# Gathering per-item adapters by indirect DMA, and another order of weight chunks, in an adapter and mixture-of-experts kernel

## The chip, the cores and the metric
One core of one Trainium2 chip runs the whole program. The metric is the device time of one execution in microseconds (us). It is lower when the kernel is better.

## The reference
The input is `x` of 64 items by 64 tokens by 256 features, float32, with two ids per item. What is computed, in order:

```
# L0: adapter
h   = gelu(x @ down_W.T + down_b)                 # 256 -> 64, erf gelu
h   = h @ expert_W[id].T + expert_b[id]           # one 64x64 adapter per item (16 adapters,
h   = h + domain_emb[id]                          #   or the identity for an invalid id)
x1  = layernorm(h @ up_W.T + up_b + x) * gamma + beta
# L1: style-conditioned mixture of experts
n   = layernorm(x1) * ln_g + ln_b
n   = (n - mean over the item's tokens) * rsqrt(var over the item's tokens)
sty = mlp(subj_emb[subject_id])                   # 64->128->128->64->512
n   = n * softplus(sty[:256]) + sty[256:]
top 2 of 8 experts by softmax(n @ router_w), gates normalised over the two
out = x1 + sum of the two of gate * (relu(n @ w1[e] + b1[e]) @ w2[e] + b2[e])   # 256->1024->256
```

## The kernel before, in words
The 4096 tokens go through a **front** in 8 groups of 512 tokens (8 items each), and then the expert layers run over **tiles** of up to 256 routed tokens (32 whole tiles and 7 half ones). The front ends where the first twelve tiles are known and their tokens lie in the DRAM tensor `queues`. A short stretch of groups 6 and 7 runs beside the first tiles.

The front is a software pipeline written out by hand, with one instruction list for each engine. `iterations(body)` runs `body` for i = 0 to 7, and `back(i, n)` is the group n iterations earlier. Iteration i does the adapter of group i, the layer norms of group i-1 (`s2`), the item norm, router and top-2 of group i-2 (`s3`), and place numbers and scatter of group i-3 (`s4`). An engine's list is strictly in order: an instruction that waits holds up all behind it on its engine.

The **expert weights** are 32 chunks of 128 x 1024 float32 (512 KB). A chunk is loaded by SP into one of four slots of `stage` (`load_weights`, L447 to L450), ScalarE writes its high half in f16 (`cut_high`, L916), and VectorE the rest (`cut_low`, L1246). SP loads chunk q when `w_low_ready` has reached q-3: chunk q-4 has to be cut by VectorE first. `CUTS` (L57) says how many chunks belong to each iteration; the last entry is the stretch behind iteration 7. In iterations 1 to 7 VectorE cuts its chunks behind `norm_shift` of group i-1. ScalarE cuts the first one ahead of `activate`, the second ahead of `adapted`, and all others ahead of `item_norm` of group i-2, which the router (PE `route`), the logits copy (ACT `logits`) and VectorE's `best_two` follow.

The **adapters** of all 64 items are made at the start: the table of 17 x 4096 is loaded, and PE's `select` (L650) multiplies it by a one-hot matrix in 32 steps. The copies (`copy_selected`) lie between the chunk cuts on ScalarE and VectorE and bring it into `wsel`. `scratch`, `table` and `wsel` lie in the room of weights that come late. The **style net** (`style_layer`, `style_out`, `softplus`, `item_gammas`) runs once, in iteration 1 and right behind it.

GpSimd does the powers of the norms (`rstd`, `item_rstd`) and the scatters: eight indirect DMAs for each group from iteration 3 on, two ahead of the second `rstd` and six behind it.

PE's order in `body` is `into_features`, `adapter` (down, adapters, up), `route`, `back_rows`, `normed_into_features`, `rank`. SP's order is the chunks of iteration i, `load_x` for group i+1 once `up_done` of group i-1 is there, and `store_x1` of group i-1.

Of the kernel before, what the change touches and what calls it, by code (L numbers as in the profile page):

```python
# [26 lines left out]
F32 = mybir.dt.float32  # L27
# [7 lines left out]
P = 128  # L35
# [21 lines left out]
CUTS = [8, 3, 3, 3, 3, 3, 3, 3, 3]  # L57
# [5 lines left out]
W2_AT = EXPERTS * DC * FF  # L63
STAGES = 4
# [80 lines left out]
def program(nc, sem, env):  # L145
# [11 lines left out]
    with ExitStack() as ctx:  # L157
# [6 lines left out]
        part_no = sb("part_no", [P, 1])  # L164
        expert_no = sb("expert_no", [P, EXPERTS])
# [63 lines left out]
        table = w_low[0:NONE_ROW + 1, 16 * CHUNK:24 * CHUNK].bitcast(F32)  # L229
        wsel = w_low[0:A, 24 * CHUNK:32 * CHUNK].bitcast(F32)  # L230
        wsel_pairs = wsel.rearrange("a (i q w) -> a w q i", q=A // 2, w=2)
# [7 lines left out]
        idf = scr(NONE_ROW + 1, ITEMS)  # L239
        sidf = scr(SUBJECTS, ITEMS)  # L240
        idc = scr(NONE_ROW + 1, ITEMS)
# [18 lines left out]
        ids_i = scr(SUBJECTS, ITEMS).bitcast(I32)  # L260
# [57 lines left out]
        ids_loaded, table_loaded = sem("ids_loaded"), sem("table_loaded")  # L318
# [3 lines left out]
        hot_ready, select_done = sem("hot_ready"), sem("select_done")  # L322
        select_copied = [sem("select_copied0"), sem("select_copied1")]
# [26 lines left out]
        N_EARLY, N_LATE = 8, 8  # L350
        N_POOL = 13
        SELECTS = A // 16

        def iterations(body, after={}):

            for i in range(GROUPS):
                body(At(i // 2, i % 2))
                if i in after:
                    after[i]()
# [73 lines left out]
        with nc.Block() as block:  # L433

            @block.sync
            def _(sp):
# [17 lines left out]
                sp.dma_start(ids_i, spread(ids, SUBJECTS)).then_inc(ids_loaded, 16)  # L454
                sp.dma_start(sids_i, spread(subject_ids, SUBJECTS)).then_inc(ids_loaded, 16)
                for dst, src in ((dw[:], down_w), (t_ab, adapter_b), (t_de, domain_emb), (t_se, subj_emb),
                                 (ab[:, 0:1], down_b), (ab[:, 1:2], sty_b1), (uw[0:A], up_w), (uw[A:A + 1], up_b)):
                    sp.dma_start(dst, src).then_inc(early_loaded, 16)
                load_weights(At(0, 0), slice(0, 2))
# [3 lines left out]
                def body(i):  # L463
# [1196 lines left out]
```

## Time and profile before

| what | value |
|---|---|
| time, median of 3 runs | 590.06 us (589.53 to 590.67) |
| the profiled execution | 590.25 us, span 588.4 us |
| PE busy | 535.2 us, 91% |
| VectorE busy | 380.0 us, 65% |
| ScalarE busy | 277.2 us, 47% |
| GpSimd busy | 244.2 us, 42% |
| DMA, mean over the span | 57.58 MB, 98 GB/s |
| first expert matmul of PE (L835) | starts at 181.35 us |

The span runs from the first to the last instruction; the time holds some 1.9 us more around it. A busy share is taken over the whole span, and the front (up to 181 us) and the expert tiles have different limits, so the share of PE says little about the front.

### The profile page before, as it was taken

Reading aid. Unit: us, or ns where it says so; the run is one execution under the profiler, and the core shown is the slowest. Engines: PE = TensorE matmul, PEld = TensorE weight load, DVE = VectorE, ACT = ScalarE, POOL = GpSimd, SP = SyncE. Lnnn points to the kernel's source line nnn. Section 1 sums busy time; section 2 is a strip of 40 time slices with the busy share of each in tenths; the row PEclk is TensorE's granted clock in tenths of the full one; section 3 lists DMA queues with packets and bytes.
Section 4 is the critical chain, followed back from the end, with each engine's and each line's share of the span. In section 5 each row is a group of like instructions: output and inputs, shape, how many; then the busy total and the mean of one; then the engine's idle time right before and its main releaser. Section 6 shows DMA issues by size and latency. Waiting matters only on the chain.

```text
span 588.4 us, 15554 instructions
## 1 busy us (share of the span) xinstructions
PE 535.2 (91%) x4386; PEld 450.1 (76%) x4387; DVE 380.0 (65%) x1233; ACT 277.2 (47%) x628; POOL 244.2 (42%) x208
## 2 busy tenths in 40 slices
PE   5987887879886999999999999999999999999991
PEld 4755654665655988888888888888888888887781
DVE  2475989888889868558865464554645546464541
ACT  3547766766663663444243342534425334254430
POOL 2000458888776625647233242322423223233222
PEclk9778789786967999899999999999999999999997
DMA  9466355775354343435655234342333424324411
GB/s 243 149 204 180 104 157 171 252 236 183 145 191 112 80 64 46 103 65 112 135 92 72 38 46 62 39 69 36 49 59 40 68 36 50 49 35 52 45 27 19
DMA packets 78094, 57.58 MB, mean 98 GB/s; under 512 B 51346, under 2 KB 71699, under 8 KB 77907
## 3 DMA queue, kind: packets, MB, share of 16 engines
q1 hardware_dynamic: 63698, 38.37, 25.6%
q0 software_dynamic: 13296, 17.83, 18.0%
q10 hardware_dynamic: 1058, 0.85, 0.7%
q8 instruction: 22, 0.36, 0.3%
q14 instruction: 20, 0.16, 0.1%
HBM read 23.18 MB, written 24.55 MB: 81 GB/s over the span
## 4 chain that ended last, share of the span: by engine, by line
PE 65%; POOL 12%; DVE 8%; issue 7%; DMA 4%; ACT 2%; SPq 1%; POOLq 0%; DVEq 0%; ACTq 0%
PE banks L835 28%; PE banks L851 27%; POOL queues L573 5%; POOL rsT L581 3%; DMA out<-nb,token 3%; PE banks L658 2%; POOL rs L564 2%; PE banks L718 2%; DVE stats L1172 2%; PE banks L719 1%; DVE w_low L1255 1%; POOL out L604 1%; PE banks L698 1%; DMA uw<-up_b 1%; PE banks L693 1%
## 5 line engine op out<-in xcount | busy, mean ns | idle before, releaser
L604 POOL DMA_INDIRECT out<-nb,token x71 | 115.6, 1628 | 224.1 <-ACT nb L1046 199.9
L835 PE MATMUL banks<-rT,w_high 128*128 128x256 f16 (+1 forms) x1248 | 198.5, 266 | 6.2 <-DMA rT<-queues 5.7
L851 PE MATMUL banks<-w_high,stage 128*128 x1136 | 188.2, 273 | 1.0 <-issue 0.5
L835 PE MATMUL banks<-rT,w_low 128*128 128x256 f16 (+1 forms) x624 | 164.2, 265 | 0.0
L851 PE MATMUL banks<-w_low,stage 128*128 x568 | 154.8, 273 | 0.0
L1030 ACT ACTIVATE xb<-banks,feat 128x256 f32<-128x256 f32 (+1 forms) x312 | 120.1, 453 | 52.3 <-PE banks L835 45.3
L835 PEld LDWEIGHTS banks<-rT,w_high 128*128 x1248 | 115.0, 99 | 25.5 <-issue 7.6
L851 PEld LDWEIGHTS banks<-w_high,stage 128*128 128x128 f16 x1136 | 110.5, 98 | 14.9 <-issue 2.3
L1046 ACT ACTIVATE nb<-act,gate 128x256 f32<-128x256 f32 x71 | 32.6, 501 | 178.7 <-DVE act L1513 174.6
L1488 DVE TENSOR_TENSOR stage<-xb,stage 128x512 f16<-128x512 f32 (+1 forms) x156 | 100.7, 646 | 5.4
L1486 DVE CAST stage<-xb 128x512 f16<-128x512 f32 (+1 forms) x156 | 67.0, 430 | 56.1 <-ACT xb L1030 54.8
L573 POOL DMA_INDIRECT queues<-h_rows,slot x64 | 75.6, 1182 | 22.5 <-issue 17.5
L1513 DVE SCALAR_TENSOR_TENSOR act<-banks,b 128x256 f32<-128x256 f32 x71 | 27.2, 420 | 86.7 <-PE banks L851 83.0
L835 PEld LDWEIGHTS banks<-rT,w_low 128*128 x624 | 61.5, 99 | 6.5
L851 PEld LDWEIGHTS banks<-w_low,stage 128*128 128x128 f16 x568 | 55.6, 98 | 6.4
L1255 DVE SCALAR_TENSOR_TENSOR w_low<-stage,w_high 128x1024 f16<-128x1024 f32 x32 | 37.6, 1222 | 2.8 <-ACT w_high L919 2.8
L562 POOL TENSOR_SCALAR rs<-mv 128x4 f32<-128x4 f32 x16 | 5.1, 319 | 71.5 <-DVE mv L1177 71.2
L919 ACT ACTIVATE w_high<-stage 128x1024 f16<-128x1024 f32 x32 | 33.4, 1052 | 2.5 <-DMA stage<-expert_w 2.5
L581 POOL TENSOR_TENSOR rsT<-varT,minus_half 128x8 f32<-128x8 f32 x16 | 27.0, 1699 | 15.6 <-DVE varT L1215 15.6
L718 PE MATMUL banks<-uw,dom 65*128 65x256 f32 x64 | 27.0, 513 | 4.8 <-ACT dom L938 4.8
L719 PE MATMUL banks<-xb,ident 128*128 128x256 f32 x64 | 25.7, 492 | 0.0
L944 ACT ACTIVATE hT<-hT,aff_c,aff_a 128x64 f32<-128x64 f32 x56 | 19.3, 427 | 7.1 <-DVE aff_c L1232 7.1
(186 smaller groups left out, 521.9 us busy)
## 6 DMA issues: line engine op xcount, KB each, us to landing
stage<-expert_w SPq DMA_DIRECT2D x32, 512.0 KB, 4.4
xb<-x SPq DMA_DIRECT2D x8, 512.0 KB, 6.1
out<-rb SPq DMA_DIRECT2D x8, 512.0 KB, 3.2
queues<-pad_row SPq DMA_DIRECT2D x9, 260.0 KB
out<-nb,token POOLq DMA_INDIRECT x71, 4.0
queues<-h_rows,slot POOLq DMA_INDIRECT x64
b<-exp_b SPq DMA_DIRECT2D x1, 1024.0 KB, 6.7
rT<-queues SPq DMA_TRANSPOSE x39
```

The costliest lines, as they stand in the source:

```text
L573: nc.gpsimd.indirect_dma_start(out=queues, out_offset=bass.IndirectOffsetOnAxis(ap=slot[:, i.par, t, k:k + 1], axis=0), in_=h_rows[:, i.pa ...
L581: nc.gpsimd.tensor_tensor(rsT[:, of_c], varT[:, of_c], minus_half[:, of_c], ALU.pow).then_inc(rsT_ready, 1)
L604: nc.gpsimd.indirect_dma_start(out=out, out_offset=bass.IndirectOffsetOnAxis(ap=token[:, i.par, s:s + 1], axis=0), in_=yg[:, i.par, s, :], ...
L718: nc.tensor.matmul(ps_u[:, t, :], dom[:, t * P:(t + 1) * P], uw[:], start=True, stop=False)
L835: last = nc.tensor.matmul(ps_in(i, c), w[:, at], features(i)[:, v, k, :], start=(n == 0), stop=(n == 3 * DC - 1))
L851: last = nc.tensor.matmul(ps_out(i.par)[:, s, :], v[:, i.par, c, s * P:(s + 1) * P], w[:, at], start=(n == 0), stop=(n == 3 * FC - 1))
L919: nc.scalar.activation(w_high[:, bass.ds(q * CHUNK, CHUNK)], stage[:, slot], ACT.Copy, scale=WSCALE).then_inc(w_high_ready, 1)
L1030: last = nc.scalar.activation(hid[:, c, 0:i.rows], ps_in(i, c), ACT.Relu, scale=1.0 / WSCALE, bias=feat[:, bass.ds(e * FC + (B1 + c), 1)])
L1046: nc.scalar.activation(yg[:, i.par, s, :], yb[:, s, :], ACT.Copy, scale=gate[:, i.par, s:s + 1]).then_inc(gated, 1)
L1255: V.scalar_tensor_tensor(w_low[:, w], stage[:, slot], WSCALE, w_high[:, w], ALU.mult, ALU.subtract).then_inc(w_low_ready, 1)
L1486: V.tensor_copy(hid_high[:, i.par, s, r], hid[:, s, r]).then_inc(split_high, 1)
L1488: V.tensor_tensor(hid_low[:, i.par, s, r], hid[:, s, r], hid_high[:, i.par, s, r], ALU.subtract).then_inc(split_low, 1)
```

## The change
1. **Adapters.** `select`, its one-hot table load and its eight copies go. VectorE works out for each of 128 partitions which row of the adapter table (1088 rows of 64) it wants (`row_no`). GpSimd gathers with 32 indirect DMAs of 128 rows of 256 B: four for each group (`GATHERS`), 16 ahead of iteration 0, 8 at the end of iterations 1 and 2 each. PE turns a group's four blocks (`turn_rows`), ScalarE copies the bank into `wsel` (`copy_adapters`).
2. **Loads.** The ids come first on ScalarE's queue. SP loads group 0's tokens, the small weights and then waits for the gathers of group 0 ahead of the first chunk. In iterations 1 and later SP loads the tokens ahead of the chunks, the first three chunks of an iteration ahead of `store_x1`, and the others behind it.
3. **Chunks** by iteration: 7, 6, 5, 3, 2, 2, 2, 2, and 3 behind, for 8 and then 3 each.
4. **Style.** VectorE's `style_out` goes ahead of `cut_low`, ScalarE's `softplus` ahead of `scale_features` and the last cuts of iteration 1, and `item_gammas` into iteration 2. The Gelu table is loaded explicitly at the start and behind `softplus`.

```diff
-CUTS = [8, 3, 3, 3, 3, 3, 3, 3, 3]
+CUTS = [7, 6, 5, 3, 2, 2, 2, 2, 3]
...
 # SP
                 load_x(At(0, 0))
...
+                sp.wait_ge(rows_loaded[0], GATHERS * 16)
                 load_weights(At(0, 0), slice(0, 2))
                 load_x(At(0, 1))
                 load_weights(At(0, 0), slice(2, STAGES))
...
-                    load_weights(i, slice(STAGES if i.g == 0 else 0, None))
-                    if (s2 := back(i, 1)) is not None:
-                        if i.g + 1 < GROUPS:
-                            sp.wait_ge(up_done, s2.g + 1)
-                            load_x(At(s2.half + 1, s2.par))
+                    s2 = back(i, 1)
+                    if s2 is not None and i.g + 1 < GROUPS:
+                        sp.wait_ge(up_done, s2.g + 1)
+                        load_x(At(s2.half + 1, s2.par))
+                    load_weights(i, slice(STAGES if i.g == 0 else 0, 3 if i.g else None))
+                    if s2 is not None:
                         store_x1(s2)
+                        load_weights(i, slice(3, None))
 # GpSimd
+                def gather(g):
+                    for n in range(g * GATHERS, (g + 1) * GATHERS):
+                        nc.gpsimd.indirect_dma_start(
+                            out=wrows[:, n * A:(n + 1) * A], out_offset=None, in_=table_rows,
+                            in_offset=bass.IndirectOffsetOnAxis(ap=row_no[:, n:n + 1], axis=0)).then_inc(rows_loaded[g], 16)
+                pool.wait_ge(rows_known, 2)
+                for g in range(4):
+                    gather(g)
...
+                    if i.g == 1 or i.g == 2:
+                        gather(2 * i.g + 2)
+                        gather(2 * i.g + 3)
 # PE
+                def turn_rows(g):
+                    pe.wait_ge(rows_loaded[g], GATHERS * 16)
+                    wait(pe, adapters_copied, g)
+                    if g == 2:
+                        pe.wait_ge(net_ready, 5)
+                    wait(pe, low_ready, g - 3)
+                    for k in range(GATHERS):
+                        n = g * GATHERS + k
+                        last = nc.tensor.transpose(banks[0:A, 4, k * PAIR:(k + 1) * PAIR], wrows[:, n * A:(n + 1) * A],
+                                                   ident[:])
+                    last.then_inc(rows_turned, 1)
...
 # PE, adapter(i): group 0 does the down matmuls first, then
                     if i.g == 0:
-                        select()
...
+                        item_rows()
+                        turn_rows(0)
...
+                        add_item_rows()
...
                     adapter(s1)
+                    if i.g + 1 < GROUPS:
+                        turn_rows(i.g + 1)
 # ScalarE
+                def copy_adapters(g):
+                    sc.wait_ge(rows_turned, g + 1)
+                    nc.scalar.activation(wsel[:, g * GI * A:(g + 1) * GI * A], banks[0:A, 4, :],
+                                         ACT.Copy).then_inc(adapters_copied, 1)
...
                     if i.g == 0:
+                        activate(s1)
+                        copy_adapters(0)
+                        adapted(s1)
+                        cut_high(i, slice(0, 4))
+                        copy_adapters(1)
+                        cut_high(i, slice(4, None))
+                        return
+                    if i.g == 1:
                         cut_high(i, slice(0, 1))
                         activate(s1)
...
+                        cut_high(i, slice(1, 2))
                         adapted(s1)
...
+                        cut_high(i, slice(2, 3))
+                        layer_norm(s2)
+                        softplus()
+                        nc.scalar.preload_act_table(ACT.Gelu)
+                        scale_features(s2)
+                        cut_high(i, slice(3, None))
+                        copy_adapters(2)
                         return
...
                     cut_high(i, slice(2, None))
                     if s3 is not None and s3.g < FIRST:
                         item_norm(s3)
+                    if 1 < i.g < GROUPS - 1:
+                        copy_adapters(i.g + 1)
                     if s2 is not None:
                         layer_norm(s2)
 # VectorE
+                link(V.tensor_copy(idf, ids_i))
+                link(V.tensor_scalar(idc, idf, -1.0, float(NONE_ROW), ALU.max, ALU.min))
+                link(V.tensor_scalar(none, idc, 0.0, float(NONE_ROW + 1), ALU.is_lt, ALU.mult))
+                link(V.tensor_tensor(idc, idc, none, ALU.add))
...
+                    V.tensor_scalar(row_no[some], of_half, part_share[some, 0:1], float(A), ALU.add,
+                                    ALU.mult).then_inc(rows_known, 1)
...
                     if i.g == 0:
-                        cut_low(i, slice(0, 1))
-                        for b in range(SELECTS):
-                            copy_selected(b)
-                            cut_low(i, slice(b + 1, b + 2))
                         row_constants()
-                        cut_low(i, slice(SELECTS + 1, None))
+                        cut_low(i, slice(None))
                         return
...
+                    if i.g == 2:
+                        item_gammas()
...
                     step(s2, norm_shift)
+                    style_step(style_out)
                     cut_low(i, slice(None))
-                    style_step(style_out)
...
-                iterations(body, after={1: item_gammas})
+                iterations(body)
```

## Rows read from the trace of the kernel before

**Rows 1.** Busy time of PE, PEld, VectorE, ScalarE, GpSimd in a stretch (start:end length), granted clock, DMA

```profile
95.10:113.70 18.60, 15.49 (x85) 12.24 (x86) 16.85 (x70) 12.17 (x24) 16.17 (x15) 0.82 0.63 212
...
132.40:152.90 20.50, 18.41 (x89) 12.55 (x88) 17.19 (x72) 12.77 (x24) 17.45 (x17) 0.72 0.59 205
...
181.30:588.00 406.70, 391.76 (x3652) 345.19 (x3652) 240.69 (x720) 168.15 (x449) 148.72 (x101) 0.98 0.39 61
```

**Rows 2.** Timeline of VectorE: start us, duration, line, operation

```profile
8.65 0.18 DVE L1114 CAST w_high<-w_high 17x64 f32<-17x64 int32 x1 [7.29 <-DMA w_high<-subject_ids]
...
39.40 1.43 DVE L1172 BATCH_NORM_STATS2 stats<-banks 128x6 f32<-128x256 f32 x4 [1.71 <-PE banks L719]
...
48.33 0.16 DVE L1199 SCALAR_TENSOR_TENSOR shift<-mv,rs 128x4 f32<-128x4 f32 x1 [1.47 <-POOL rs L564]
...
51.81 0.47 DVE L1155 TENSOR_SCALAR w_high<-banks,feat 128x64 f32<-128x64 f32 x2
...
59.03 1.43 DVE L1172 BATCH_NORM_STATS2 stats<-banks 128x6 f32<-128x256 f32 x4
...
69.73 0.16 DVE L1199 SCALAR_TENSOR_TENSOR shift<-mv,rs 128x4 f32<-128x4 f32 x1 [0.33 <-POOL rs L564]
...
73.22 0.37 DVE L1262 MAX8 top<-lg 128x8 f32<-128x8 f32 x4
...
76.40 1.42 DVE L1172 BATCH_NORM_STATS2 stats<-banks 128x6 f32<-128x256 f32 x4
...
107.12 3.50 DVE L1255 SCALAR_TENSOR_TENSOR w_low<-stage,w_high 128x1024 f16<-128x1024 f32 x3
```

**Rows 3.** Timeline of TensorE, same columns

```profile
13.08 1.94 PE L693 MATMUL banks<-ident,item_add 128*64 128x512 f32 x2 [0.53 <-DVE w_high L1128]
...
18.02 11.20 PE L658 MATMUL banks<-w_high,w_low 17*128 17x64 f32 x64
...
33.27 1.22 PE L718 MATMUL banks<-uw,dom 65*128 65x256 f32 x2 [0.68 <-ACT dom L938]
...
38.77 0.59 PE L719 MATMUL banks<-xb,ident 128*128 128x256 f32 x2
...
146.59 0.96 PE L719 MATMUL banks<-xb,ident 128*128 128x256 f32 x2
```

**Rows 4.** Timeline of ScalarE, same columns

```profile
18.71 1.04 ACT L919 ACTIVATE w_high<-stage 128x1024 f16<-128x1024 f32 x1
...
32.63 0.59 ACT L938 ACTIVATE dom<-banks 64x512 f32<-64x512 f32 x1 [2.07 <-PE banks L710]
...
53.52 1.45 ACT L978 ACTIVATE hT<-banks,feat 128x512 f32<-128x512 f32 x2 [2.92 <-PE banks L753]
...
54.86 0.31 ACT L910 ACTIVATE w_high<-w_high 128x128 f32<-128x128 f32 x1
...
58.10 0.31 ACT L914 ACTIVATE w_high<-w_high 128x128 f32<-128x128 f32 x1
...
66.79 2.76 ACT L944 ACTIVATE hT<-hT,aff_c,aff_a 128x64 f32<-128x64 f32 x8 [0.94 <-DVE aff_c L1232]
...
69.93 2.08 ACT L964 ACTIVATE nb<-rb,shift,rs 128x256 f32<-128x256 f32 x4 [0.38 <-DVE shift L1199]
```

**Rows 5.** Timeline of GpSimd, iteration 4, behind the second rstd

```profile
107.17 2.13 POOL L573 DMA_INDIRECT queues<-h_rows,slot  x1 [0.20 <-issue]
...
109.61 1.86 POOL L573 DMA_INDIRECT queues<-h_rows,slot  x1 [0.30 <-issue]
...
111.77 0.96 POOL L573 DMA_INDIRECT queues<-h_rows,slot  x1 [0.31 <-issue]
```

**Rows 6.** DMA issues: size, median us from issue to landing

```profile
out<-nb,token POOLq DMA_INDIRECT x71, 4.0
...
w_high<-subject_ids SPq DMA_DIRECT2D x1, 8.0 KB, 6.9
```

**Rows 7.** Source line L450, the 32 chunk loads

```profile
DMA to landing us min/median/max: 3.2/4.4/9.0
```

More of the change, by code:

```diff
@@ L63 @@
 W2_AT = EXPERTS * DC * FF
+ROWS_AT = CHUNKS - GROUPS // 2
+ADAPTERS_AT = ROWS_AT - GROUPS
+PAIR = 2 * A
+GATHERS = GROUP // T // 2
 STAGES = 4
@@ L259, in program @@
         lnz = scr(P, DC * ITEMS)
[L260 removed]
+        ids_i = scr(P, ITEMS).bitcast(I32)
         sids_i = scr(SUBJECTS, ITEMS).bitcast(I32)
@@ L648, in item_rows @@
                     nc.tensor.matmul(banks[0:SE, 7, A:A + ITEMS], t_se, hot_s, start=True, stop=True).then_inc(net_done, 1)
-                def select():
-                    pe.wait_ge(table_loaded, 32)
-                    for b in range(SELECTS):
-                        for w in range(2):
-                            wait(pe, select_copied[w], b - 1)
-                        for k in range(8):
-                            q = b * 8 + k
-                            last = nc.tensor.matmul(banks[:, 4 + b % 2, k * ITEMS:(k + 1) * ITEMS],
-                                                    table[:, q * 2 * A:(q + 1) * 2 * A], hot_w, start=True, stop=True)
-                        last.then_inc(select_done, 1)
+                def turn_rows(g):
[9 more added lines that the diff above has]
+                    last.then_inc(rows_turned, 1)
                 def style_layer(k):
@@ L1013, in body @@
                         scale_features(s2)
-                sc.dma_start(table[0:ADAPTERS], adapter_w[0:ADAPTERS]).then_inc(table_loaded, 16)
-                sc.dma_start(table[ADAPTERS:NONE_ROW + 1].rearrange("o (k n) -> o k n", k=16),
-                             adapter_w[ADAPTERS:NONE_ROW + 1].rearrange("o (k n) -> o k n", k=16)).then_inc(table_loaded, 16)
-                for dst, src in ((hw1, hyp_w1), (feat[:], feature), (hw2, hyp_w2), (sw1, sty_w1), (sw2, sty_w2),
-                                 (g0[:], spread(gamma0, P)), (b0[:], spread(beta0, P)), (rw[:], router_w)):
-                    sc.dma_start(dst, src).then_inc(late_loaded, 16)
-                iterations(body, after={1: softplus})
+                sc.dma_start(ids_i, spread(ids, P)).then_inc(ids_loaded, 16)
+                sc.dma_start(sids_i, spread(subject_ids, SUBJECTS)).then_inc(ids_loaded, 16)
+                nc.scalar.preload_act_table(ACT.Gelu)
+                for dst, src in ((t_ab, adapter_b), (t_de, domain_emb), (t_se, subj_emb), (ab[:, 1:2], sty_b1)):
+                    sc.dma_start(dst, src).then_inc(early_loaded, 16)
+                iterations(body)
                 cut_high(last_chunks, slice(None))
@@ L1447, in body @@
                     step(s3, row_fields)
-                iterations(body, after={1: item_gammas})
+                iterations(body)
                 def late_tiles():
```

100 lines of the change are left out of this document (47 added, 53 removed).

## The prediction

> **What bounds the kernel now.** I read the stretches first. In the expert tiles TensorE is busy 391.8 of 406.7 us at a granted clock of 0.98 [rows 1]; the change touches no tile, so this part is fixed and the question is only when it starts. The front gives that start: PE's first tile matmul waits for tokens that SP fetches once VectorE has the table of tiles, and VectorE makes this table at the end of iteration 7. So I follow VectorE's list through the front. I mark an iteration by the first `stats` of group i-1 (L1172): iteration 1 begins at 39.40, 2 at 59.03, 3 at 76.40 [rows 2], and 4 at the left edge of the stretch 95.1:113.7 [rows 1].
>
> Three different limits show. Up to 39.40 it is one chain: VectorE has the ids at 8.65 [rows 2], PE's `select` takes 11.20 us from 18.02, the last copy into `wsel` ends at 29.25 + 1.30 = 30.55 [rows 3, 4], then come the adapter matmuls, ScalarE's copy `dom` at 32.63, and the sixteen up matmuls from 33.27 [rows 3, 4]. In iterations 1 and 2 it is VectorE's own list with one wait for the softplus. From iteration 4 on GpSimd has no rest: 16.17 us busy in 18.60 [rows 1], and the eight gaps of 0.30 us between its scatters [rows 5] are issue time, not waiting. VectorE is nearly as full (16.85) and waits for GpSimd's second power once in each iteration.
>
> The sum is made against the profiled execution, 590.25 us; the median of the runs, 590.06, lies 0.2 us lower.
>
> **The start (to iteration 1).** `select` and its copies go. The gathers take their place, and all of the following is in series.
> - Ids: 6.9 us from issue to landing [rows 6], issued some 0.5 us earlier (two issues ahead of it on SP fall away). By that 8.1; as the table load no longer shares the queues, it can be sooner. I take 7.5 (5.2 to 8.1).
> - Six small VectorE operations of 0.18 and a little [rows 2]: 1.3, so 8.8.
> - Four gathers. No gather is in the trace. The nearest row is a scatter of 128 rows: 0.96 us by itself, 2.13 beside a chunk cut, 0.30 between two [rows 5]. No cut runs yet, so I take 0.96: 4 x 0.96 + 3 x 0.30 = 4.7, so 13.6. Bounds 0.96 and 2.13 each.
> - Landing: the indirect DMA of the tiles takes 4.0 us from its issue [rows 6]; from the last gather's issue at 12.6 that is 16.6; its own issue is shorter, so I take 16.0.
> - PE turns the four blocks (1.0 at half clock) and adds the item rows, 1.94 [rows 3]: 18.9. ScalarE's copy of 0.6, of the shape of `dom` [rows 4], lies beside it.
> - From here as before: 30.55 to 39.40, 8.85 us: `up_done` at 27.8.
> - New behind it: `turn_rows(1)` 0.5, `copy_adapters(1)` 0.6, and ScalarE's last three cuts of iteration 0, which now stand behind that copy, 3 x 1.04 [rows 4], and VectorE's last cut 1.2 (3.50 for three [rows 2]). Iteration 1 begins at 33.2.
>
> That is 6.2 us sooner than 39.40. The chunks themselves start late, since SP waits for group 0's gathers (16.0 where it was 6.6), but a load takes 3.2 to 4.4 us [rows 7] and ScalarE is not free for the first cut before 21.6; this wait is covered. SP has the first four chunks and the tokens of group 1 behind it, and PE needs those only after 27.8.
>
> **Iteration 1 (6 chunks for 3).** It was 59.03 - 39.40 = 19.6, with VectorE idle for the softplus. Now VectorE has `style_out` ahead of the cuts (two pairs of 0.47 [rows 2]) and no wait there, but ScalarE makes chunks 10 to 12 only behind the whole style chain. Path: `norm_shift` 48.33 - 39.40 = 8.95 [rows 2]; `layer_norm` 2.3 with its start; softplus from 54.86 to 58.41, 3.55; the Gelu table 1.28; `scale_features` 1.45; three cuts 3.1 [rows 4]; VectorE's last one 1.2. Sum 21.8: **+2.2**.
>
> **Iteration 2 (5 chunks for 3).** Here I expect the main loss. Chunks 13 to 17; a chunk's load waits until the chunk four before it is cut by VectorE. So 13 to 16 come early, but 17 waits for VectorE's cut of 13, which stands behind `norm_shift`. And ScalarE's `item_norm`, `layer_norm`, `logits` and `high` stand behind its cut of 17. Before, `item_norm` ran at 66.79, 3 us ahead of `norm_shift` at 69.73 [rows 2, 4]. Now: `norm_shift` at 10.7 plus 0.6 for `item_gammas`, 11.3. Then VectorE's cut 1.2, load 4.0 (3.2 to 4.4 [rows 7]), ScalarE's cut 1.04, `item_norm` 2.76, `copy_adapters` 0.6, `layer_norm` 2.1, the logits copy 0.2, and VectorE from `best_two` to the next `stats` 76.40 - 73.22 = 3.2 [rows 2, 4]. That is 15.2, where it was 76.40 - 69.73 = 6.7. The iteration is 26.5 for 17.4: **+9.1** (bounds 8.3 to 13, the longest loads and a half-clock PE for the router).
>
> **Iteration 3** has 3 chunks as before; `copy_adapters` takes 0.6 us in front of `layer_norm` where ScalarE had idled 1.4 us for VectorE's shift: **+0.1**. PE's `turn_rows`, 0.5 us, lies in PE's wait for `item_norm`.
>
> **Iterations 4 to 6 (2 chunks for 3).** VectorE saves 1.17 each. GpSimd sets the pace: beside 3.50 us of cuts two scatters took 2.13 + 1.86 instead of 2 x 0.96 [rows 2, 5], 2.07 lost, 0.6 us for each us of cuts. A third less is 0.7. **-0.7 each, -2.1** (bounds 0 to -1.17 each). **Iteration 7**: VectorE saves 1.17, but GpSimd's last scatters, which SP waits for also, save only 0.7: **-0.9**.
>
> The gathers of iterations 1 and 2, eight each behind the second `rstd`: 8 x 1.26 = 10.1, and 0.6 x 3.5 for the cuts beside them, twice at most: 14.3. They start 9.0 into iteration 1 and end by 23.3; the next `rstd` is due 1.9 into iteration 2, 23.7. Cost 0, by a hair.
>
> The shared port gets a rule in the Trainium skill (page "SBUF — State Buffer", section "SBUF: two separate sides"): a VectorE instruction that holds the port pair blocks GpSimd fully, not in part. The rows give 0.6, not 1. By the rule the gathers of iteration 1 would lose 7.0 instead of 4.2.
>
> **Sum.** -6.2 + 2.2 + 9.1 + 0.1 - 2.1 - 0.9 = **+2.2**: 592.4 for the profiled execution, about 592.3 for the median. Slower.
>
> **Rivals.**
> 1. *The start gains more than the stalls cost* (faster). Its place is the chain to 33.2. If the ids land at 5.2 (-2.3), and PE is at the full clock for the up matmuls (two take 0.59 at 38.77 against 1.22 at 33.27 [rows 3], so 3.5 for 6.1, -2.6) and for the turn (-0.5), iteration 1 begins at 27.8 and the time is 592.4 - 5.4 = 587.0. It decides if iteration 1 begins before 31 us. For it: the queue is lighter. Against it: PE rests from 12 to 16 us and was at half clock after such rests.
> 2. *The slow stretch goes.* Iteration 6 took 20.5 us at a granted clock of 0.72 [rows 1]: its up matmuls ended at 147.55 and ScalarE waited for the router. If the clock falls elsewhere, the iteration is 18.0 and gains 2.5 instead of 0.7: 590.6, no change that can be told.
> 3. *The new copy makes the slow stretch worse.* `layer_norm` now stands behind `copy_adapters`, which waits for PE behind its up matmuls. With those ending at 147.55 [rows 3]: turn 1.0, copy 0.6, `layer_norm` 2.1, so the logits copy at 151.3 instead of 149.3, +2.1, and the 0.7 is lost also: 592.4 + 2.8 = 595.2.
> 4. *GpSimd is late with its gathers.* At a full block in iteration 1 (both sets of three cuts, 7.0 us) the gathers end at 26.1 into it, 2.4 after the next `rstd` is due: 594.8. For it: one gather's price is unknown. (It is the port rule above that gives this.)
>
> **How the numbers follow.** Forecast 0.42, rival 1 0.25, rival 2 0.15, rival 3 0.12, rival 4 0.06. A change below 0.2%, 1.2 us, can't be told from none here. The forecast, rivals 3 and 4 are slower, 0.60, less the forecast's low edge of 0.02; rival 2 with that edge is 0.17; rival 1 is 0.25. The forecast's own range is 590.8 to 595. The whole range takes in rival 1's 587.0 and rival 3's 595.2 with the unknown prices of the load and the gather (3 us up if each gather of the first group takes 2.13 and a chunk load longer): 586 to 598.
>
> **What would show it.** In the changed trace: iteration 1's `stats` near 33 us (before 31: rival 1). In iteration 2 ScalarE idle for a chunk load, `item_norm` some 6 us behind `norm_shift` instead of ahead; `stats` of iteration 3 near 81.5, later than 76.40. Iterations 4 and 5 near 18.0 us long. If `item_norm` of group 0 isn't behind the shift, the main term is wrong. If GpSimd's `rstd` starts later than VectorE's moments in iteration 2, rival 4 holds.

## The result, and the profile after

The changed kernel takes 595.50 us (median of 5 runs, 591.68 to 599.32), the kernel before 589.74 us beside it (5 runs, 588.94 to 590.67). The ratio is 1.010, with a 95% interval of 1.0066 to 1.0133: slower, by 5.8 us in the medians. The forecast was 592.3, in a range of 586 to 598. All ratios here and below compare fast executions only; four of the 70 of the kernel before in the experiments were slow ones and stand in its medians, but not in the ratios.

The profiled execution of the changed kernel is the longest of its five, 599.32 us, and its span is 9.1 us longer than the span before. I compare the two fronts first. The marks are the same as in the prediction: an iteration begins at the first `stats` of VectorE, and the front ends at the first tile matmul.

| begins at (us) | it. 1 | it. 2 | it. 3 | it. 4 | it. 5 | it. 6 | it. 7 | first tile | end of span |
|---|---|---|---|---|---|---|---|---|---|
| before | 39.4 | 59.0 | 76.4 | 95.1 | 113.7 | 132.4 | 152.8 | 181.35 | 588.4 |
| after | 33.0 | 57.7 | 85.8 | 104.4 | 123.3 | 140.9 | 158.45 | 186.30 | 597.5 |
| after - before | -6.4 | -1.3 | +9.4 | +9.4 | +9.6 | +8.5 | +5.7 | +4.95 | +9.1 |

The front is 4.95 us longer, and that is near the 5.8 us between the medians. The other 4.2 us lie in the tiles (411.2 us for 407.0), which the change doesn't touch. In the ten profiled runs of the experiments, all with the same instructions in the tiles, this part took 406.6 to 410.8 us, 409.1 in the mean. About half of the 4.2 us is thus the spread of single executions. The other half, by which that mean lies above 407.0, may be spread of the one profile of before: the kernel before with nothing but the new chunk numbers also took 409.25. Whether any of it belongs to the change is open.

The page of the changed kernel, with its busy times, three of its groups (busy us, mean ns of one, idle before and what ended it) and the chunk loads (KB each, us to landing):

```profile
span 597.5 us, 15538 instructions
PE 527.9 (88%) x4354; PEld 443.4 (74%) x4355; DVE 376.0 (63%) x1233; ACT 275.4 (46%) x631; POOL 274.8 (46%) x240
L1302 DVE SCALAR_TENSOR_TENSOR w_low<-stage,w_high 128x1024 f16<-128x1024 f32 x32 | 37.7, 1220 | 20.0 <-ACT w_high L953 20.0
L597 POOL DMA_INDIRECT w_low<-adapter_w,row_no x32 | 34.8, 1088 | 13.1 <-issue 9.2
L953 ACT ACTIVATE w_high<-stage 128x1024 f16<-128x1024 f32 x32 | 33.1, 1050 | 15.1 <-DMA stage<-expert_w 15.1
stage<-expert_w SPq DMA_DIRECT2D x32, 512.0 KB, 5.4
```

The L953 row is the first hint. ScalarE was idle for 15.1 us because a chunk had not landed, 10.3 of them in iteration 2. VectorE was idle for 20.0 us because ScalarE had not cut; 10.2 of these lie ahead of its very first cut. GpSimd has 30.6 us more work than before, and no wait of that kind stands at it.

The timeline of VectorE after, which answers to [rows 2] (start, duration, line, operation, idle before):

```profile
6.62 0.20 DVE L1163 CAST w_high<-w_high 128x64 f32<-128x64 int32 x1 [4.90 <-DMA w_high<-subject_ids]
...
32.98 1.42 DVE L1220 BATCH_NORM_STATS2 stats<-banks 128x6 f32<-128x256 f32 x4
...
41.35 0.28 DVE L1197 TENSOR_SCALAR w_high<-banks,ab 64x64 f32<-64x64 f32 x1 [2.68 <-PE banks L694]
...
44.83 0.16 DVE L1247 SCALAR_TENSOR_TENSOR shift<-mv,rs 128x4 f32<-128x4 f32 x1 [1.48 <-POOL rs L574]
...
54.28 3.50 DVE L1302 SCALAR_TENSOR_TENSOR w_low<-stage,w_high 128x1024 f16<-128x1024 f32 x3 [5.12 <-ACT w_high L953]
57.70 1.41 DVE L1220 BATCH_NORM_STATS2 stats<-banks 128x6 f32<-128x256 f32 x4
...
68.93 0.16 DVE L1247 SCALAR_TENSOR_TENSOR shift<-mv,rs 128x4 f32<-128x4 f32 x1 [0.33 <-POOL rs L574]
69.01 4.62 DVE L1302 SCALAR_TENSOR_TENSOR w_low<-stage,w_high 128x1024 f16<-128x1024 f32 x4
75.11 1.23 DVE L1302 SCALAR_TENSOR_TENSOR w_low<-stage,w_high 128x1024 f16<-128x1024 f32 x1 [1.48 <-ACT w_high L953]
81.64 0.37 DVE L1309 MAX8 top<-lg 128x8 f32<-128x8 f32 x4 [5.29 <-ACT lg L985]
...
84.26 1.23 DVE L1334 TENSOR_TENSOR h_rows<-banks,h_rows 128x1024 f16<-128x1024 f32 x1 [0.88 <-ACT h_rows L992]
```

Two waits stand out. In iteration 1 VectorE is idle for 5.12 us, until ScalarE comes to the last three chunks. In iteration 2 it is idle for 5.29 us, until the logits are there. ScalarE shows why (answers to [rows 4]):

```profile
30.75 1.06 ACT L953 ACTIVATE w_high<-stage 128x1024 f16<-128x1024 f32 x1 [0.61 <-DMA stage<-expert_w]
...
51.86 1.45 ACT L1012 ACTIVATE hT<-banks,feat 128x512 f32<-128x512 f32 x2
53.20 2.94 ACT L953 ACTIVATE w_high<-stage 128x1024 f16<-128x1024 f32 x3
...
69.21 1.06 ACT L953 ACTIVATE w_high<-stage 128x1024 f16<-128x1024 f32 x1 [6.58 <-DMA stage<-expert_w]
74.03 1.06 ACT L953 ACTIVATE w_high<-stage 128x1024 f16<-128x1024 f32 x1 [3.76 <-DMA stage<-expert_w]
74.99 2.75 ACT L978 ACTIVATE hT<-hT,aff_c,aff_a 128x64 f32<-128x64 f32 x8
...
81.41 0.20 ACT L985 ACTIVATE lg<-banks 128x32 f32<-128x32 f32 x1 [1.23 <-PE banks L763]
```

The three cuts of iteration 1 (53.20) stand behind the whole style chain and `scale_features` (51.86). In iteration 2 the cut at 74.03 is chunk 17's. Its load could be issued only when VectorE had cut chunk 13, the first of the four at 69.01. `item_norm` (L978) stands behind it at 74.99, where before it ran at 66.79, ahead of VectorE's shift [rows 4].

Chunk 16, the cut at 69.21, was late as well, for another reason. The change puts the fourth and fifth chunk of an iteration behind `store_x1` in SP's list, and the store of group 1 waits until VectorE has finished the group's first layer norm. SP after:

```profile
64.52 0.40 SPq L450 DMA_DIRECT2D out<-rb  x1
64.95 5.63 SPq L455 DMA_DIRECT2D stage<-expert_w  x2
```

The second row holds the loads of chunk 16, at 64.95, and of chunk 17, at the end of its 5.63 us. Chunk 12, whose slot chunk 16 takes, was cut at 57.8, so the load of 16 waited some 7 us for the store. Without chunk 17 `item_norm` would still have stood behind this cut, at 70.3, though ScalarE was free from 62.6 on and VectorE had the last of its coefficients at 67.8. By these rows the place of the store would then cost 2.5 us or more; that is my estimate.

PE after (answers to [rows 3]):

```profile
14.90 1.06 PE L684 MATMUL banks<-ident,w_low 128*64 128x128 f32 x4 [4.25 <-DMA w_low<-adapter_w,row_no]
...
26.00 0.60 PE L684 MATMUL banks<-ident,w_low 128*64 128x128 f32 x4
...
35.12 0.66 PE L694 MATMUL banks<-w_high 128*128 128x64 f32 x2 [6.37 <-DVE w_high L1191]
...
37.47 3.62 PE L726 MATMUL banks<-xT,dw 128*64 128x512 f32 x4
...
77.79 3.58 PE L763 MATMUL banks<-rw,hT 128*128 128x8 f32 x16 [7.82 <-ACT hT L978]
```

Both long rows, 37.47 and 77.79, come behind a rest of PE (6.37 and 7.82 us). The same work of the same group in the kernel before took half as long, so these rows are at the lower of TensorE's two levels, 1.2 GHz, and those of before at 2.4:

```profile
42.80 1.88 PE L698 MATMUL banks<-xT,dw 128*64 128x512 f32 x4
...
70.21 1.85 PE L732 MATMUL banks<-rw,hT 128*128 128x8 f32 x16
```

GpSimd after (answers to [rows 5]):

```profile
8.37 1.20 POOL L597 DMA_INDIRECT w_low<-adapter_w,row_no  x1 [3.90 <-DVE row_no L1170]
...
12.39 0.95 POOL L597 DMA_INDIRECT w_low<-adapter_w,row_no  x1 [0.30 <-issue]
...
59.62 0.23 POOL L572 TENSOR_SCALAR rs<-mv 128x4 f32<-128x4 f32 x1 [3.29 <-DVE mv L1225]
...
69.08 2.12 POOL L597 DMA_INDIRECT w_low<-adapter_w,row_no  x1 [0.18 <-issue]
71.50 1.82 POOL L597 DMA_INDIRECT w_low<-adapter_w,row_no  x1 [0.30 <-issue]
...
116.57 2.11 POOL L583 DMA_INDIRECT queues<-h_rows,slot  x1 [0.20 <-issue]
118.99 0.97 POOL L583 DMA_INDIRECT queues<-h_rows,slot  x1 [0.30 <-issue]
```

And the stretches of iterations 2, 4, 5, 6 and of the tiles after, with the columns of [rows 1]:

```profile
57.70:85.80 28.10, 17.62 (x84) 14.64 (x83) 19.66 (x72) 13.87 (x24) 15.90 (x14) 0.64 0.49 167
...
104.40:123.30 18.90, 16.30 (x90) 12.01 (x90) 15.85 (x70) 11.99 (x24) 16.17 (x16) 0.82 0.44 145
123.30:140.90 17.60, 14.71 (x90) 10.83 (x90) 15.84 (x71) 12.04 (x25) 14.44 (x14) 0.90 0.69 239
140.90:158.40 17.50, 14.72 (x90) 10.83 (x90) 15.73 (x69) 11.95 (x24) 15.07 (x15) 0.90 0.54 175
...
186.30:597.50 411.20, 394.48 (x3652) 347.07 (x3652) 239.34 (x719) 168.69 (x449) 148.08 (x100) 0.97 0.38 60
```

No engine is full in iteration 2: VectorE, the busiest, has 19.66 of 28.10 us. It is a stretch of waits, and the granted clock is 0.64 in it.

### The profile page after: what moved, and what is told of

It reads as the page before. It is cut to its first block, busy times and chain, and to the rows that moved or that the text cites. A ratio compares the mean times of both kernels' runs of the same rounds, so it can differ in the third digit from the quotient of the medians.

```text
span 597.5 us, 15538 instructions
## 1 busy us (share of the span) xinstructions
PE 527.9 (88%) x4354; PEld 443.4 (74%) x4355; DVE 376.0 (63%) x1233; ACT 275.4 (46%) x631; POOL 274.8 (46%) x240
## 4 chain that ended last, share of the span: by engine, by line
PE 59%; POOL 12%; DVE 9%; issue 7%; DMA 7%; ACT 4%; SPq 0%; ACTq 0%; POOLq 0%; DVEq 0%
PE banks L869 28%; PE banks L885 27%; POOL queues L583 5%; DMA out<-nb,token 3%; POOL rsT L591 3%; DMA stage<-expert_w 3%; POOL rs L574 2%; DVE w_low L1302 2%; DVE stats L1220 2%; POOL out L628 1%; PE banks L763 1%; DMA w_high<-subject_ids 1%; PE banks L726 1%; POOL rs L572 1%; PE banks L749 1%
## 5 line engine op out<-in xcount | busy, mean ns | idle before, releaser
L869 PEld LDWEIGHTS banks<-rT,w_high 128*128 x1248 | 115.4, 99 | 28.1 <-issue 9.4
L885 PEld LDWEIGHTS banks<-w_high,stage 128*128 128x128 f16 x1136 | 110.5, 98 | 14.7 <-issue 1.9
L583 POOL DMA_INDIRECT queues<-h_rows,slot x64 | 72.5, 1133 | 22.5 <-issue 17.2
L1558 DVE SCALAR_TENSOR_TENSOR act<-banks,b 128x256 f32<-128x256 f32 x71 | 27.1, 420 | 87.6 <-PE banks L885 85.9
L597 POOL DMA_INDIRECT w_low<-adapter_w,row_no x32 | 34.8, 1088 | 13.1 <-issue 9.2
L953 ACT ACTIVATE w_high<-stage 128x1024 f16<-128x1024 f32 x32 | 33.1, 1050 | 15.1 <-DMA stage<-expert_w 15.1
L749 PE MATMUL banks<-uw,dom 65*128 65x256 f32 x64 | 29.5, 557 | 5.9 <-ACT dom L972 4.1
L750 PE MATMUL banks<-xb,ident 128*128 128x256 f32 x64 | 27.7, 527 | 0.0
L749 PEld LDWEIGHTS banks<-uw,dom 65*128 65x128 f32 x64 | 17.4, 283 | 10.5 <-ACT dom L972 5.0
```

The lines of the kernel that those rows point to most:

```text
L583: nc.gpsimd.indirect_dma_start(out=queues, out_offset=bass.IndirectOffsetOnAxis(ap=slot[:, i.par, t, k:k + 1], axis=0), in_=h_rows[:, i.pa ...
L597: nc.gpsimd.indirect_dma_start(out=wrows[:, n * A:(n + 1) * A], out_offset=None, in_=table_rows, in_offset=bass.IndirectOffsetOnAxis(ap=ro ...
L749: nc.tensor.matmul(ps_u[:, t, :], dom[:, t * P:(t + 1) * P], uw[:], start=True, stop=False)
L869: last = nc.tensor.matmul(ps_in(i, c), w[:, at], features(i)[:, v, k, :], start=(n == 0), stop=(n == 3 * DC - 1))
L885: last = nc.tensor.matmul(ps_out(i.par)[:, s, :], v[:, i.par, c, s * P:(s + 1) * P], w[:, at], start=(n == 0), stop=(n == 3 * FC - 1))
L953: nc.scalar.activation(w_high[:, bass.ds(q * CHUNK, CHUNK)], stage[:, slot], ACT.Copy, scale=WSCALE).then_inc(w_high_ready, 1)
```

## Experiments

Ten kernels. Each median stands beside that of the kernel before on the same chip. A single profiled execution differs from the next by 1 or 2 us in a mark even where the instructions up to it are the same (iteration 1 of the changed kernel began at 33.0, 34.0 and 34.3 in three such runs), so I read marks to about that.

### One chunk fewer in iteration 2

```diff
-CUTS = [7, 6, 5, 3, 2, 2, 2, 2, 3]
+CUTS = [7, 6, 4, 3, 3, 2, 2, 2, 3]
```

> The changed kernel with one chunk moved from iteration 2 to iteration 4: CUTS 7, 6, 4, 3, 3, 2, 2, 2, 3. Theory (the fifth chunk of iteration 2 can load only after VectorE has cut the first, and ScalarE's item_norm stands behind it): ScalarE no longer waits for the load of chunk 17, item_norm of group 0 starts near 70.3 us instead of 75.0, iteration 3 begins near 80 instead of 85.8, and iteration 4 is 0.9 longer. Time 590.5, some 5 us below the changed kernel's 595.5. Rival (the loss in iteration 2 is the amount of cutting on VectorE, or PE at half clock, whatever the order): one chunk, 1.2 us less in iteration 2, given back in iteration 4: 595.

Measured: 590.58 us (10 runs) for 590.46, ratio 1.0001 (0.9973 to 1.0028). Iteration 2 took 23.4 us (58.7 to 82.2) instead of 28.1. With four chunks the last load of the iteration waits for no cut behind the shift. Moving the fifth chunk brings the time back to that of the kernel before. It doesn't bring iteration 2 back to its 17.4 us: ScalarE still waits 5.38 us for chunk 16, whose load stands behind `store_x1`, and `item_norm` starts only at 71.4. No run here has that load ahead of the store with four chunks, so its price is open.

### The chunks as before, all the rest of the change kept

```diff
-CUTS = [7, 6, 5, 3, 2, 2, 2, 2, 3]
+CUTS = [8, 3, 3, 3, 3, 3, 3, 3, 3]
```

> The changed kernel with the old chunk numbers 8, 3, 3, 3, 3, 3, 3, 3, 3 and all else of the change. Theory: the gathers and the new load order gain some 6 us at the start and only the chunk numbers lose it again in iterations 1 and 2: iteration 2 begins near 51, iteration 3 near 70 (76.4 in the kernel before), later iterations are 0.9 longer than in the changed kernel: time 583.5, faster than before by some 6 us. Rival (what the change adds besides the chunks, the gathers on GpSimd, the turns on PE and the copies in ScalarE's list, eats the gain): 590 or more.

Measured: 588.96 us (10 runs) for 590.46, ratio 0.9979 (0.9948 to 1.001). The interval holds 1, so a gain isn't shown, and in the medians it is far smaller than I expected, 1.5 us. The profiled execution looks better: its first tile matmul comes at 175.88, 5.5 us sooner than before. But at 586.98 us it is one of the fastest of its ten runs. Iterations 2 and 3 took 22.0 and 20.7 us. VectorE and then GpSimd in this run:

```profile
53.34 1.67 DVE L1253 BATCH_NORM_STATS2 statsT<-hT 128x6 f32<-128x128 f32 x8 [1.76 <-ACT hT L1012]
58.32 1.67 DVE L1241 SCALAR_TENSOR_TENSOR rb<-rb,rs,b 128x256 f32<-128x256 f32 x4 [1.68 <-POOL rs L574]
...
78.35 1.67 DVE L1241 SCALAR_TENSOR_TENSOR rb<-rb,rs,b 128x256 f32<-128x256 f32 x4 [1.37 <-POOL rs L574]
```

```profile
55.94 0.94 POOL L597 DMA_INDIRECT w_low<-adapter_w,row_no  x1 [0.30 <-issue]
56.91 0.24 POOL L572 TENSOR_SCALAR rs<-mv 128x4 f32<-128x4 f32 x1
```

Iteration 1 is only 14.7 us long here (35.0 to 49.75), and the last gather ends at 56.88. The `rstd` that VectorE needs starts right behind it, at 56.91, with no idle time before it. (The first row above is another delay, ScalarE's `scale_features` behind the softplus.) This is rival 4's place, but not its cause: the gathers end about 22 us into iteration 1, near the 23.3 of the prediction's sum, but the iteration that had to cover them had become 10 us shorter.

### Chunk 17's high cut behind layer_norm in iteration 2

```diff
-                    cut_high(i, slice(2, None))
+                    cut_high(i, slice(2, 4 if i.g == 2 else None))
...
+                    if i.g == 2:
+                        cut_high(i, slice(4, None))
```

> The changed kernel with the same chunk numbers, but in iteration 2 ScalarE cuts the fifth chunk (17) behind layer_norm instead of ahead of item_norm. Theory (the order on ScalarE, not the number of chunks, makes the stall): item_norm starts near 70.3, the cut of 17 near 76, iteration 3 begins near 81.5 instead of 85.8: time 591. Rival (number of chunks): no difference, 595.

Measured: 591.32 us (10 runs) for 590.46, ratio 1.0035 (1.0003 to 1.0067); iteration 3 begins at 81.6, and iteration 2 took 23.3 us for 28.1. The number of chunks is the changed kernel's; only ScalarE's order differs. So these 4.8 us aren't the fifth chunk's work (1.04 us on ScalarE, 1.17 on VectorE), but `item_norm` behind a load that waits for VectorE. The iteration is still 5.9 us longer than before; ScalarE waits 4.89 us for chunk 16 here too, and `item_norm` starts at 70.8.

### Only the new chunks, on the kernel before

```diff
-CUTS = [8, 3, 3, 3, 3, 3, 3, 3, 3]
+CUTS = [7, 6, 5, 3, 2, 2, 2, 2, 3]
```

> The kernel before with the new chunk numbers 7, 6, 5, 3, 2, 2, 2, 2, 3 alone. Theory: in iteration 1 and in iteration 2 ScalarE's layer_norm or item_norm waits for chunks (12 and 17) that load only after VectorE's first cut of that iteration; two stalls of 7 to 9 us each, less 1 us at iteration 0 and 3 us in iterations 4 to 7: 600 to 605. Rival (front-loading is free by itself, and the loss comes with the gathers or the load order): 587 to 590.

Measured: 602.88 us (4 runs) for 590.46, ratio 1.0204 (1.0145 to 1.0262). Iteration 1 took 27.1 us and iteration 2 27.9. ScalarE in iteration 2:

```profile
82.38 1.06 ACT L919 ACTIVATE w_high<-stage 128x1024 f16<-128x1024 f32 x1 [9.08 <-DMA stage<-expert_w]
```

The same wait for the same chunk, without any gather in the program. Here all five loads stand ahead of the store, and only chunk 17 is late. In iteration 1 ScalarE waited 3.92 and 2.46 us for chunks 11 and 12. The table of chunks costs 12.4 us by itself; beside it the rest of the change gives 6 to 7 us back. The two don't simply add up: without the new table the rest gave only 1.5 us in the medians.

### Old chunks, gathers spread

Five groups are gathered ahead (for four), group 5 between the two `rstd` of iteration 1, groups 6 and 7 at the end of iterations 1 and 2.

```diff
-CUTS = [7, 6, 5, 3, 2, 2, 2, 2, 3]
+CUTS = [8, 3, 3, 3, 3, 3, 3, 3, 3]
...
-                for g in range(4):
+                for g in range(5):
...
+                    if i.g == 1:
+                        gather(5)
...
-                        gather(2 * i.g + 2)
-                        gather(2 * i.g + 3)
+                        gather(i.g + 5)
```

> The changed kernel with the old chunk numbers and the gathers placed otherwise: five groups ahead of iteration 0, one between the two rstd of iteration 1, one at the end of iterations 1 and 2 each (eight at the end of each before). Theory (in short iterations the eight gathers end after the next rstd is due, the mechanism of the prediction's rival 4: with old cuts VectorE waited for GpSimd 1.7 us in iteration 2 and 1.4 + 2.3 us in iteration 3): these waits go, iteration 3 begins near 70.3 instead of 71.8 and lasts 18.7 instead of 20.8, time 585.5, 3.5 below the 589.0 of the old cuts alone. Rival (the wait only hides another, ScalarE's late logits of group 0): 588 to 589.

Measured: 587.41 us (11 runs) for 589.63, ratio 0.9954 (0.9925 to 0.9983): faster than both kernels. GpSimd now idles ahead of the `rstd` of iteration 2:

```profile
55.75 0.23 POOL L572 TENSOR_SCALAR rs<-mv 128x4 f32<-128x4 f32 x1 [1.96 <-DVE mv L1226]
```

Iteration 3 takes 18.4 us (72.4 to 90.8) for 20.7 with all eight gathers at the end. Iteration 1 takes 17.9 for 14.7, as PE's up matmuls ran at the lower clock (two in 1.06 us, from 46.69 to 53.79) where they had run at the full one. In the profiled executions the first tile matmul comes only 0.4 us sooner than with the old chunks alone, and the intervals of the two ratios overlap. That the waits for GpSimd go is shown; that the spreading pays in time isn't. Its median lies 1.9 us above what I expected, and its first tile matmul comes 5.9 us sooner than before (175.49) for 2.2 us between the medians. The profiled execution, 583.98 us, is near the low end of its 11 runs (583.52 to 589.49), so its marks show more than the median gives. What makes single executions of one kernel differ by 6 us is open; the mean granted clocks of these 11 (0.932 to 0.948) don't order them by time.

### New chunks, gathers spread

The same edit of the gathers, on the changed kernel.

> The changed kernel with its own chunk numbers and the gathers placed as in the run before this one. Theory: with the new chunk numbers iterations 1 and 2 are so long that the gathers end before the next rstd is due (56.3 against 59.6, and 80.9 against 87.7 in the changed kernel), so nothing changes: 595. Rival (the gathers cost the changed kernel something, by the port or by DMA beside the chunk loads): 592 or less.

Measured: 595.52 us (6 runs) for 589.63, ratio 1.0115 (1.0065 to 1.0165), the changed kernel's own time (1.010). So in the changed kernel the gathers cost nothing on GpSimd, and rival 4 is out for it. Beside the run before this one, the chunks alone are worth 595.52 - 587.41 = 8.1 us.

### Old chunks, chunk loads ahead of the tokens again

```diff
-CUTS = [7, 6, 5, 3, 2, 2, 2, 2, 3]
+CUTS = [8, 3, 3, 3, 3, 3, 3, 3, 3]
...
+                    load_weights(i, slice(STAGES if i.g == 0 else 0, 3 if i.g else None))
                     if s2 is not None and i.g + 1 < GROUPS:
                         sp.wait_ge(up_done, s2.g + 1)
                         load_x(At(s2.half + 1, s2.par))
-                    load_weights(i, slice(STAGES if i.g == 0 else 0, 3 if i.g else None))
```

> The changed kernel with the old chunk numbers and, in iterations 1 and later, the first chunks loaded ahead of the tokens again. Theory (tokens are needed a whole iteration after they are asked for, so their order is covered): as with the old cuts alone, 589, iteration starts the same within 0.5 us. Rival (chunks that stand behind up_done come late to ScalarE): 1 to 3 us faster.

Measured: 590.15 us (11 runs) for 589.63, ratio 1.0019 (0.9984 to 1.0055). Against 0.9979 for the same kernel with tokens first the two intervals overlap. Inconclusive: what the order on SP is worth isn't told apart from nothing. The marks missed my 0.5 us: iteration 1 began at 35.15 for 35.02, but iteration 2 at 52.8 for 49.75. The up matmuls of iteration 1 ran at the lower clock here too. GpSimd shows something that the changed kernel doesn't, a gather that lasted through all that was left of three cuts (VectorE's, 47.25 to 50.73):

```profile
47.94 3.62 POOL L597 DMA_INDIRECT w_low<-adapter_w,row_no  x1 [0.30 <-issue]
```

### No wait for the rows ahead of the first chunk

```diff
-                sp.wait_ge(rows_loaded[0], GATHERS * 16)
```

> The changed kernel without SP's wait for the gathers of group 0 ahead of the first chunk; chunks and tokens of group 1 load from 7.7 us on. Theory (the wait costs nothing, as ScalarE has no time for the first cut before 20.3 us, and it keeps the gathers from sharing the DMA engines with 2.5 MB): the gathers of group 0 land 0 to 2 us later than 14.9 us, iteration 1 begins at 33 to 35, time 595 to 597. Rival (the late chunks hold up ScalarE's cuts 4 to 6 and so the start of iteration 1, where it idled 0.6 to 0.9 us before each): iteration 1 begins near 31, time 593.

Measured: 599.6 us (5 runs) for 589.63, ratio 1.0173 (1.0131 to 1.0215), and iteration 1 begins at 36.4. GpSimd's last gather of group 0 and then PE's first turn:

```profile
12.54 0.95 POOL L596 DMA_INDIRECT w_low<-adapter_w,row_no  x1 [0.30 <-issue]
```

```profile
18.21 1.06 PE L683 MATMUL banks<-ident,w_low 128*64 128x128 f32 x4 [6.40 <-DMA w_low<-adapter_w,row_no]
```

The rows land 18.21 - 12.54 = 5.7 us after the start of the last gather. With the wait it was 14.90 - 12.39 = 2.5. Chunks were under way beside them from 7.87 us on. So the wait, which looks like a delay of 7 us for the chunks (first issue at 14.87 for 7.87), gives 2 to 3.4 us at iteration 1 (33.0 to 34.3 with it) and some 4 between the medians, though the intervals of the two ratios just overlap. I had put it at 0 to 2 us, and the rows came 3.3 us later, so both my theory and my rival missed.

### Style layer 2 behind the down matmuls

On the kernel with old chunks and spread gathers; PE runs `style_layer(2)` behind the four down matmuls of group 1 instead of ahead of its item rows.

```diff
 # PE, adapter, behind the down matmuls
                     if i.g == 1:
+                        style_layer(2)
                         style_layer(3)
...
-                    if i.g == 1:
-                        style_layer(2)
```

> The kernel with old chunk numbers and spread gathers (587.4), and in iteration 1 PE's second style layer issued behind the down matmuls of group 1 instead of ahead of them. In that kernel PE rests some 6 us for VectorE's first style copy and then runs the down matmuls at half clock, and iteration 2 begins 2.1 us late for up_done of group 1. Theory: the down matmuls start some 2 us earlier, iteration 2 begins near 52 instead of 53.8, time 585.5. Rival (VectorE then waits as long for the second layer, or ScalarE's router chain of group 0 sets iteration 3 anyway): 587.4.

Measured: 586.21 us (12 runs) for 589.82, ratio 0.9952 (0.9922 to 0.9981), the fastest kernel of this study, though it can't be told from the one it is built on. VectorE and then PE:

```profile
40.74 0.27 DVE L1197 TENSOR_SCALAR w_high<-banks,ab 64x64 f32<-64x64 f32 x1
```

```profile
34.00 3.39 PE L727 MATMUL banks<-xT,dw 128*64 128x512 f32 x4 [4.54 <-ACT xT L960]
```

In the changed kernel VectorE waited 2.68 us for style layer 3 at this place; that wait is gone. The down matmuls are still at the lower clock (3.39 us for four), but they no longer stand behind style layer 2, which waits for VectorE's first style copy of the iteration: they start 0.6 us ahead of iteration 1, where the run it is built on had them 4.5 us into it (40.45 for 35.95). Iteration 1 takes 14.5 us (34.6 to 49.2) for 17.9. Part of that may be the clock of the up matmuls, as the old chunks alone had 14.7 us without this edit.

### A fourth chunk in iteration 1, on the same

```diff
-CUTS = [8, 3, 3, 3, 3, 3, 3, 3, 3]
+CUTS = [8, 4, 3, 3, 3, 3, 3, 2, 3]
```

> As the run before this one, with chunk numbers 8, 4, 3, 3, 3, 3, 3, 2, 3: four chunks in iteration 1 all fit the four slots, so no load waits for a cut of the same iteration. Theory: iteration 1 no longer (VectorE has slack there), iteration 7 0.7 to 0.9 shorter: 0.8 us below d1. Rival (any chunk more in iteration 1 lengthens ScalarE's list there by 1.04, and so iteration 2): the same or up to 0.5 above d1.

Measured: 589.26 us (12 runs) for 589.82, ratio 0.9989 (0.9962 to 1.0017). VectorE at the end of iteration 1:

```profile
55.38 1.23 DVE L1302 SCALAR_TENSOR_TENSOR w_low<-stage,w_high 128x1024 f16<-128x1024 f32 x1 [5.12 <-ACT w_high L953]
```

My theory, that the fourth chunk is free there, fell, and so did the rival with its 0.5 us at most: the median is 3.05 us above the run before, though the intervals of the two ratios overlap a little. ScalarE cuts it only behind `layer_norm`, the softplus with its three table loads, and `scale_features`; iteration 1 grew from 14.5 to 20.5 us (36.1 to 56.5). This is the changed kernel's wait in iteration 1, 5.12 us in both, with one chunk instead of three: the price is the place in ScalarE's list, not the number of chunks.

## Why the prediction was right, by its steps

The sign, the range and the main mechanism held. The sum of the front was too small: +2.2 forecast, +4.95 in the profiled front. The median of 595.5 lies in the whole range, but 0.5 us above the forecast's own 590.8 to 595. It lies next to rival 3's 595.2 and rival 4's 594.8, but neither explains it: rival 4 was absent, and rival 3's mechanism cost 1.3 us at most (below). The profiled execution, against which the sum was made, came 9.1 us later and not 2.2, outside the range; 4.2 of that lie in the tiles, which the sum took as fixed.

| step | forecast | measured |
|---|---|---|
| start | -6.2 | -6.4 |
| iteration 1 | +2.2 | +5.1 |
| iteration 2 | +9.1 | +10.7 |
| iteration 3 | +0.1 | 0.0 |
| iteration 4 | -0.7 | +0.3 |
| iteration 5 | -0.7 | -1.1 |
| iteration 6 | -0.7 | -2.8 |
| iteration 7 to the first tile | -0.9 | -0.7 |

**Start.** The end is right to 0.2 us, the way to it partly by luck. The ids landed sooner (6.62 for 7.5), the first gather started at 8.37 for 8.8, the last one of group 0 ended at 13.34 for 13.6, and the rows landed at 14.90 for 16.0. PE had done the up matmuls at 26.0 (its turn of group 1 starts there), 1.8 us ahead of my 27.8. But I had called the chunk loads "covered", and they weren't: ScalarE's last two cuts of iteration 0 waited 0.91 and 0.61 us for their loads, and the cut at 30.75 set iteration 1. The first load was issued only at 14.87, and a load took 5.4 us at the median where I had taken 3.2 to 4.4 [rows 7]; chunk 6 could load only when VectorE had cut chunk 2, at 25.14. What the gathers gave, the chunks took. And the profiled 33.0 is the lowest of three starts with the same instructions (33.0, 34.0, 34.3). Rival 1 had both its conditions in part (early ids, PE at full clock from 24.7 us on) and failed for this reason; it needed iteration 1 before 31 us.

**Iteration 1**, the term that failed most, by 2.9 us, all of it ahead of the shift. I had kept 8.95 us from `stats` to `norm_shift`; it took 44.83 - 32.98 = 11.85. Since PE was done early and VectorE was late with its chunk cuts, PE rested for 6.37 us, ran style layer 2, then the down matmuls in 3.62 us at the lower clock, and VectorE waited 2.68 us for style layer 3 queued behind them. With layer 2 moved behind the down matmuls the wait was gone. From the shift to iteration 2 I had 12.85 us (softplus, table, `scale_features`, three cuts, VectorE's cut), and 57.70 - 44.83 = 12.87 were measured.

**Iteration 2**, the main term. Up to the shift 11.23 us for 11.3. My sentence that chunks 13 to 16 come early was wrong for chunk 16: its load stood behind `store_x1` and landed at 69.21. In the changed kernel chunk 17 hid this. Behind the shift every link is in the trace: VectorE's cut of chunk 13 from 69.01, chunk 17 landed at 74.03, `item_norm` 74.99, `layer_norm` 78.12, logits 81.41, next `stats` 85.80. That is 16.9 us for 15.2. The difference is PE again: the router took 3.58 us behind a rest of 7.82, so the logits copy waited 1.23 us for it, and VectorE another 0.88 for the copy of what PE turned next. I had named a half-clock router as a bound and not put it in the sum. With 17 cut later, 4.8 us of the iteration went (23.3 for 28.1), and with one chunk fewer 4.7. The other 6 us of the 10.7 stayed in both runs, with ScalarE idle for chunk 16 for 4.9 and 5.4 us of them; how much of the 6 the store's place made, no run tells.

**Iterations 3 to 7.** Iteration 3 as forecast. In iterations 4 to 7 the sum was -3.0 and -4.4 was measured. Where GpSimd set the pace a chunk fewer gave 1.1, not 0.7: beside two cuts only one scatter was lengthened (2.11, then 0.97), where it had been two (2.13 and 1.86 [rows 5]). Iteration 6 gave 2.8, since its slow stretch (clock 0.72 before [rows 1]) ran at 0.90: rival 2 happened, but as a part of the sum and not in place of it. Iteration 4 gave nothing, and there rival 3's mechanism did occur. Its up matmuls ran at the lower clock to 117.0, PE turned the adapters behind them, and ScalarE's `copy_adapters` waited for it:

```profile
117.48 0.59 ACT L1018 ACTIVATE w_low<-banks 64x512 f32<-64x512 f32 x1 [2.32 <-PE banks L684]
```

`layer_norm` followed at 117.97, 1.4 us behind VectorE's shift, where before it started as soon as the shift was there (107.20), and VectorE waited 1.29 us for the logits. The router ended only at 119.13, so without the copy the logits would have come some 0.8 us sooner (my estimate from these rows). Rival 3 had priced this at 2.1 us, in iteration 6.

**Rival 4** was absent in the changed kernel (GpSimd idle for 3.29 us ahead of `rstd`, and spreading the gathers changed nothing), and present as soon as the chunks were put back. The gathers of iteration 1 ended 23.35 us into it (56.33), the 23.3 of my sum, but by two errors that cancel: they started 3 us later than I had it, and took 11.35 us for 14.3. The price of cuts to gathers was mostly 0.44 to 0.49 us for each us of cuts: 2.04 us lost on two gathers beside 4.62 us of cuts, and 1.15 on one scatter beside two cuts of 1.17. Two gathers ended inside that stretch of 4.62 us. In two runs (tokens behind the chunks, and no wait for the rows) it was more: one gather took 3.62 us and ended 0.8 us behind the last of three cuts, 2.67 lost beside 2.8 us of them. The Trainium skill ("SBUF — State Buffer", section "SBUF: two separate sides") gives the port pair to one instruction for the whole of its time, with the other engine fully blocked. The 2.12 us of the first gather agree with one such block, 0.95 and one cut of 1.17. That a block lasts through a whole stretch of cuts, as I had read it for the 7.0 us, agrees with the 3.62 us and not with the two gathers of iteration 2. What decides between the two, no run shows.

## What to carry to other kernels

A buffer ring ties a load to the cut of the buffer one turn before. Before giving a stage more chunks than the ring has slots, follow the last load back: if it waits for a late instruction of the stage, or stands in its queue behind a store that does, everything queued behind that chunk on its engine waits too, and a chunk of 1 us can cost 5. Ask of every chunk at which place of the slowest engine's list it is handled, since that place and not the engine's busy time is its price. And when one part of a change shortens a stretch that covered another, check the cover again: the gathers were free in an iteration of 24.7 us and in the way in one of 14.7.

## What the runs showed of the hardware

- An indirect gather of 128 rows of 256 B holds GpSimd for 0.95 us and 0.30 to the next, the first one 1.20. The data of four were there 2.5 us after the start of the last with no chunk load under way, and after 5.7 us beside loads of 512 KB.
- Beside VectorE's cuts a gather took up to 2.12 us instead of 0.95 in eight of the ten kernels with gathers, and 3.62 us once in each of the other two.
- PE came back at the lower clock after rests of 6.37 and 7.82 us: the same router took 3.58 us, and before the change 1.85, right behind the up matmuls. How long it stayed there varied: behind a rest of 7.36 us (old chunks alone) the up matmuls of iteration 1 ran at the full clock, behind one of 8.53 (gathers spread) at the lower one.
- Executions of one kernel spread by up to 1.5% (583.15 to 591.89 us over 22 runs of the kernel before). A single profile beside a single profile would have shown 9.1 us here, where the medians differ by 5.8.
